# Gate stage of a graph network: one accumulator, eight places for gathered rows, loops of two turns, and an end without GpSimd

## The chip, the cores and the metric

One core of a Trainium2 chip runs the whole program. Its engines are TensorE (PE), VectorE (DVE), ScalarE (ACT), GpSimd (POOL) and SyncE (SP), each with its own stream of instructions; they meet at semaphores. The metric is the device time of one execution in microseconds; lower is better.

## The reference, cut to what matters

Four graph layers are applied one after the other to 6250 nodes of 128 features, with 100000 edges sorted by their target. The change touches the last one only, the gated layer:

```python
xr, xc = x[row], x[col]                       # source and target of each edge
x_src = xr @ W_src + b_src
x_dst = xc @ W_dst + b_dst
x_edge = concatenate([xr, xc]) @ W_edge + b_edge
gates = softmax(concatenate([x_src, x_dst, x_edge]) @ W_gate + b_gate)   # three gates of an edge
out = gates[:, 0:1] * x_src + gates[:, 1:2] * x_dst + gates[:, 2:3] * x_edge
result = x + segment_sum(out, col)            # summed by target node
```

## The kernel before

The stage before the loop computes, for each node, two vectors of 128 features and four logits (`p_gate`), and SyncE stores them as rows of 260 numbers in the table `tab_gate` in device memory. Then TensorE computes the products that belong to the target side (`p_gate_dst`, matmuls at line 1031, taken from PSUM by VectorE at line 1064), and the gate loop follows.

**The loop.** Edges are handled in steps of 128, four steps (`U`) are a part, four parts (`PARTS`) a turn. There are 52 turns, so 208 parts. `edge_loop` writes each engine's loop: a list of pairs (lag, step), run for each part, where a step with lag k handles the part that lies k parts back. The first turn is written out, 51 turns are a hardware loop (`Fori`), and the late parts are written out again. For each part:

- GpSimd (`gate_pool`, helper `gathers`, line 409) gathers the four steps' rows from `tab_gate` by source index, one indirect transfer for 128 rows, into `rows`. It has four places of a part, and the gathers of part n wait for `gate_msg` of part n - 4.
- SyncE loads the factors of the edges' places (`gate_sp`).
- TensorE (`gate_pe`) makes the one-hot matrices from them (`turn`, lines 1917 and 1919), multiplies the target logits by them (`logits`, line 1931, lag 1), and sums the messages into PSUM (`sums`, line 448, lag 3).
- ScalarE (`gate_act`) copies the one-hots out of PSUM (lines 1894 and 1897), takes exponentials (1888) and scales one half of the row (`scale`, 1902).
- VectorE (`gate_dve`) adds the gathered logits to the target ones (`logits`, line 1946, lag 2), forms the message of the part before (`message`, line 1969, lag 3), which posts `gate_msg`, divides the gates (`gates`, lag 2), and adds the four sums out of PSUM to the nodes' blocks (`step_add`, line 471, lag 4). It executes these in this order for each part.

**The two accumulators.** `Sums` adds even steps to `acc_flat` and odd steps to `h_flat`, the memory where the rows for the table stood. Two adds that follow each other could hit the same block, so an add waits for the completed ones before it; with two accumulators only every second add has such a wait:

```python
for u in range(U * at_once):
    if u % m == 0:
        dve.wait_ge(sem("win_added"), self.added0 + TURN + n + u)
```

where `m` is the number of accumulators. Both are cleared beforehand (line 2448, in the stage before, and line 1973).

**The end.** The nodes' blocks are handled in seven groups of seven blocks. VectorE adds the two accumulators (line 1982). ScalarE scales `t` by the second gate's sum (line 1851, 49 activations). GpSimd scales `w` by the third gate's sum and adds `x` (lines 2004 and 2008). VectorE adds the one term (1987) and the other (1990) and the group is stored.

The attention stage, two layers earlier, has a loop of the same kind. Its gathers (line 1350) go to eight places of a part (`KV_RING`), and wait for VectorE's line 1600.

Of the kernel before, what the change touches and what calls it, by code (L numbers as in the profile page):

```python
# [6 lines left out]
P = 128  # L7
# [10 lines left out]
U = 4  # L18
PARTS = 4
# [75 lines left out]
def edge_loop(engine, stages, turns=TURNS):  # L95


    for r in range(PARTS):
        for lag, step in stages:
            if r >= lag:  # L100
                step((r - lag) // PARTS, (r - lag) % PARTS)
    with engine.Fori(1, turns) as i:
        for r in range(PARTS):
            for lag, step in stages:
                back = (r - lag) // PARTS
                step(i + back if back else i, (r - lag) % PARTS)
    for late in range(max(lag for lag, _ in stages)):
        for lag, step in stages:
            if late < lag:
                step(turns + (late - lag) // PARTS, (late - lag) % PARTS)  # L110
# [35 lines left out]
def program(nc, a, out):  # L146
# [6 lines left out]
    with ExitStack() as ctx:  # L153
# [244 lines left out]
        GATHER_TURNS = (TURNS, TURNS)  # L398
        TURN0 = [sum(GATHER_TURNS[:k]) for k in range(len(GATHER_TURNS))]

        def gathers(pool, k, table, width, sources, free):

            for n in range(GATHER_TURNS[k] * PARTS):
                r = n % PARTS
                if n >= PARTS:
                    free(n - PARTS)
                for u in range(U):
                    at = n * U + u
                    pool.indirect_dma_start(rows[:, r * U + u, 0:width], None, table,  # L409
                                            bass.IndirectOffsetOnAxis(sources[:, at:at + 1], 0)).then_inc(rows_in[r], 16)  # L410

        class Sums:
# [24 lines left out]
            def step_pe(self, pe, message, arrived):  # L441
                def step(i, r):
# [9 lines left out]
            def step_add(self, dve, at_once=1):  # L452
# [5 lines left out]
                def step(i, r):  # L458
# [19 lines left out]
        ATT_PASS, GATE_PASS = 0, 1  # L478
        gate_sums = Sums(1, GATE_W, 4, 2, (acc_flat, h_flat))
# [449 lines left out]
        def group(v, g):  # L929
            return v[:, ds(g * GROUP, GROUP), :]  # L930
# [229 lines left out]
        ATT_TURN0 = TURN0[ATT_PASS]  # L1160
# [710 lines left out]

        def gate_pool(pool):
# [3 lines left out]
            gathers(pool, GATE_PASS, tab_gate, GATE_ROW, src_col, lambda n: pool.wait_ge(sem("gate_msg"), n + 1))  # L1876

        def gate_sp(sp):
            def load(i, r):
# [5 lines left out]
        def gate_act(act):  # L1885
            def exp(i, r):
# [3 lines left out]
            def copy(i, r):  # L1890
# [8 lines left out]
            def scale(i, r):  # L1899
                act.wait_ge(sem("gates_ready"), i * PARTS + r + 1)  # L1900
                for u in range(U):
                    last = nc.scalar.activation(scaled[:, u, :], rows[:, r * U + u, D:KV], ACT.Copy,  # L1902
# [9 lines left out]
        def gate_pe(pe):  # L1912
            def turn(i, r):
# [9 lines left out]
            def logits(i, r):  # L1923
# [16 lines left out]
        def gate_dve(dve, chain):  # L1940
            def logits(i, r):
# [3 lines left out]
                dve.wait_ge(rows_in[r], 16 * U * (GATE_TURN0 + i + 1))  # L1945
                nc.vector.tensor_tensor(z, banks(2 + r % RING2)[:, 0:4 * U].rearrange("p (u c) -> p u c", c=4),
                                        rows[:, r * U:(r + 1) * U, KV:GATE_ROW], ALU.add).then_inc(sem("gate_step"), 1)
# [6 lines left out]
            def gates(i, r):  # L1954
# [9 lines left out]
            def message(i, r):  # L1964
                n = i * PARTS + r
                dve.wait_ge(sem("gate_scaled"), n + 1)
                for u in range(U):
                    m = r * U + u
                    last = nc.vector.scalar_tensor_tensor(msg_gate[:, m, 0:D], rows[:, r * U + u, 0:D], msg_gate[:, m, D:D + 1],  # L1969
                                                          scaled[:, u, :], ALU.mult, ALU.add)  # L1970
                last.then_inc(sem("gate_msg"), 1)
            for flat in (acc_flat, h_flat):
                nc.vector.memset(flat[:, BLOCKS * D:BLOCKS * GATE_W], 0.0).then_inc(sem("gate_zeroed"), 1)
            dve.wait_ge(sem("gate_zeroed"), 2 * GROUPS + 2)
# [5 lines left out]
            sums, sums2 = by_block(acc_flat, BLOCKS, GATE_W), by_block(h_flat, BLOCKS, GATE_W)  # L1980
            with dve.Fori(0, GROUPS) as g:
                nc.vector.tensor_tensor(group(sums, g), group(sums, g), group(sums2, g), ALU.add).then_inc(sem("gates_summed"), 1)
# [520 lines left out]
```

## Time and profile before

| | |
|---|---|
| median of 3 runs | 6562.92 us (6562.47 to 6567.48) |
| profiled execution, its time | 6606.33 us |
| its span, first to last instruction | 6604.7 us |
| TensorE busy | 4142.5 us (63%) |
| VectorE busy | 2841.6 us (43%) |
| GpSimd busy | 2539.1 us (38%) |
| ScalarE busy | 1248.9 us (19%) |
| mean granted TensorE clock | 0.726 |

Times within the profile count from the first instruction's start. A row of a timeline gives start, duration, engine, line, operation, the tensors written and read, and in brackets the idle time before it with what ended it; "issue" is a wait for nothing that the profile shows, "remote" is a release by something it cannot name. The gate stage takes about the last 1470 us of the span.

### The profile page before, as it was taken

The page shows a single profiled execution, that of the slowest core. Times are in us where ns is not written, and L with a number is a line of the kernel's source. Part 1 is how long each engine was busy: PE and PEld are TensorE (multiplying, and loading weights), DVE is VectorE, ACT ScalarE, POOL GpSimd, SP SyncE. Part 2 cuts the span into 40 slices and gives each one's busy share as a digit, 9 for nine tenths or more (in the row PEclk, how much of TensorE's full clock was granted, in tenths as well). Part 3 has the DMA queues.
Part 4 walks back from the last instruction along what each step waited for, and adds up shares of the span by engine and source line. Part 5 has one row for each costly group of instructions (what it writes and reads, how often), then busy time and mean ns, then how long its engine had stood idle before and what let it go on. Part 6 is the DMA issues. An engine that isn't in the chain of part 4 may idle for free.

```text
span 6604.7 us, 89916 instructions
## 1 busy us (share of the span) xinstructions
PE 4142.5 (63%) x24308; PEld 3118.6 (47%) x24309; DVE 2841.6 (43%) x9274; ACT 1248.9 (19%) x3117; POOL 2539.1 (38%) x2543
## 2 busy tenths in 40 slices
PE   0000000059999965777777772999998777777765
PEld 0000000036656664666666652666666666666654
DVE  4343333451131144666666667313213444444446
ACT  0000000100010021222222223101001233333333
POOL 6677666300000035555556530000000455555555
PEclk6555555579999987888888875999999655555555
DMA  9811111035555445666666551455564232332222
GB/s 359 302 44 45 45 38 51 7 116 191 191 173 190 160 122 166 189 181 180 186 186 191 177 171 42 152 191 164 181 192 142 77 81 79 81 81 80 81 80 68
DMA packets 547602, 897.05 MB, mean 136 GB/s; under 512 B 99459, under 2 KB 401573, under 8 KB 541111
## 3 DMA queue, kind: packets, MB, share of 16 engines
q1 hardware_dynamic: 429558, 614.86, 29.2%
q0 software_dynamic: 106912, 224.30, 12.7%
q10 hardware_dynamic: 10912, 55.32, 2.3%
q8 instruction: 95, 1.56, 0.1%
q14 instruction: 125, 1.02, 0.1%
HBM read 734.69 MB, written 159.48 MB: 135 GB/s over the span
## 4 chain that ended last, share of the span: by engine, by line
PE 50%; issue 19%; DVE 14%; another core or an unknown queue 11%; ACT 3%; DVEq 2%; DMA 1%; SPq 1%; ACTq 0%; POOL 0%; POOLq 0%
PE ps L840 25%; DVE work L636 4%; PE ps L1931 4%; PE ps L1489 3%; PE ps L448 3%; PE ps L1502 3%; PE ps L1491 3%; PE ps L1031 2%; PE ps L1462 1%; DVE work L1969 1%; PE ps L847 1%; PE ps L1917 1%; PE ps L1468 1%; ACT work L1902 1%
## 5 line engine op out<-in xcount | busy, mean ns | idle before, releaser
L409 POOL DMA_INDIRECT work<-tab_gate,src_col x832 | 792.4, 952 | 1863.7 <-DMA tab_gate<-logits 1247.2
L1350 POOL DMA_INDIRECT work<-tab_kv,src_col x624 | 647.1, 1037 | 1656.1 <-PE ps L1031 1137.7
L515 POOL DMA_INDIRECT d_adj<-logits,address x782 | 779.3, 997 | 364.1 <-issue 239.9
L840 PE MATMUL ps<-hw 128*128 128x384 bf16 x5096 | 856.7, 328 | 41.6 <-DVE hw L819 34.1
L840 PE MATMUL ps<-hw,work 128*128 128x384 bf16 x5096 | 845.1, 326 | 0.0
L2226 PE MATMUL ps<-work 128*128 128x49 f32 x2 | 0.6, 418 | 1230.1 <-DVE work L2323 1230.1
L840 PEld LDWEIGHTS ps<-hw 128*128 128x128 bf16 x5096 | 500.7, 98 | 369.4 <-issue 33.7
L840 PEld LDWEIGHTS ps<-hw,work 128*128 128x128 bf16 x5096 | 498.8, 98 | 318.2
L885 DVE TENSOR_TENSOR work<-work,ps 128x128 f32 (+1 forms) x208 | 59.7, 287 | 1286.6 <-ACT work L872 1285.9
L2226 PEld LDWEIGHTS ps<-work 128*128 128x128 f32 x2 | 0.5, 313 | 1230.4 <-issue 1230.4
L448 PE MATMUL ps<-work 128*128 128x132 f32 x1664 | 436.5, 443 | 121.3 <-issue 75.1
L636 DVE SCALAR_TENSOR_TENSOR work<-hw,acc 128x256 bf16<-128x256 f32 x784 | 345.9, 484 | 310.9 <-issue 297.8
L448 PEld LDWEIGHTS ps<-work 128*128 128x128 f32 x1664 | 384.8, 334 | 124.7 <-issue 124.7
L1931 PEld LDWEIGHTS ps<-logits,work 128*128 128x128 f32 x1664 | 370.2, 327 | 42.3 <-issue 42.3
L1931 PE MATMUL ps<-logits,work 128*128 x1664 | 388.0, 356 | 0.2
L872 ACT ACTIVATE work<-ps 128x128 f32 x208 | 57.6, 277 | 1683.4 <-PE ps L840 1683.4
L1564 DVE TENSOR_TENSOR acc<-acc,ps 128x136 f32 x832 | 240.0, 288 | 231.9 <-remote 142.8
L1902 ACT ACTIVATE work<-work 128x128 f32<-128x128 f32 x832 | 265.7, 390 | 272.9 <-DVE work L1961 185.4
L1489 PE MATMUL ps<-weights,work 128*128 128x128 f32 x1664 | 304.6, 339 | 12.9 <-issue 11.5
L1489 PEld LDWEIGHTS ps<-weights,work 128*128 128x128 f32 x1664 | 259.6, 238 | 78.0 <-issue 78.0
L1917 PE MATMUL ps<-step_rows,node_factors 6*128 6x512 bf16 x208 | 124.8, 600 | 269.6 <-ACT work L1897 246.4
L1491 PE MATMUL ps<-t,work 128*128 x1664 | 279.1, 321 | 17.8 <-issue 17.8
(435 smaller groups left out, 6221.2 us busy)
## 6 DMA issues: line engine op xcount, KB each, us to landing
hw<-d_adj SPq DMA_DIRECT2D x104, 800.0 KB, 4.3
work<-d_adj SPq DMA_DIRECT2D x104, 800.0 KB, 4.4
d_adj<-acc SPq DMA_DIRECT2D x52, 1568.0 KB
hw<-d_adj SPq DMA_DIRECT2D x104, 768.0 KB, 4.2
work<-d_adj SPq DMA_DIRECT2D x104, 768.0 KB, 4.3
work<-attr_dram SPq DMA_DIRECT2D x832, 64.0 KB
hw<-d_keys ACTq DMA_DIRECT2D x49, 1024.0 KB
hw<-d_value SPq DMA_DIRECT2D x192, 256.0 KB
```

The source lines that it names most:

```text
L409: pool.indirect_dma_start(rows[:, r * U + u, 0:width], None, table, bass.IndirectOffsetOnAxis(sources[:, at:at + 1], 0)).then_inc(rows_in[ ...
L448: nc.tensor.matmul(self.place(r, u), hot[:, r * U + u, :], message(r, u), start=True, stop=True).then_inc(sem("win_done"), 1)
L515: pool.indirect_dma_start(d_adj, bass.IndirectOffsetOnAxis(address[:, tile:tile + 1], 0), counts[:, tile:tile + 1], None).then_inc(adj_out ...
L636: ins = nc.vector.scalar_tensor_tensor(same[:, k, :], key_rows[:, half, k // 2, :], key_col[:, at], weigh[:, k % 2, :], ALU.is_equal, ALU. ...
L840: last = nc.tensor.matmul(at, adj_half[2 * s + hf][:, k, :], xs[:, b, :], start=b == 0, stop=b == BLOCKS - 1)
L1350: pool.indirect_dma_start(kv_rows[r][:, at % U, :], None, tab_kv, bass.IndirectOffsetOnAxis(src_col[:, at:at + 1], 0)).then_inc(rows_in[r] ...
L1489: nc.tensor.matmul(e[:, u * D:(u + 1) * D], attr_t[:, r % RING2, u * D:(u + 1) * D], weight("L1_We"), start=True, stop=True)
L1491: last = nc.tensor.matmul(q[:, u * D:(u + 1) * D], hot_t[:, r % RING2, u * P:(u + 1) * P], t[:, ds(blocks[u], 1), :].rearrange("p b f -> p ...
L1502: nc.tensor.matmul(sum_place(6, u), hot_sum[:, r * U + u, :], msg_att[:, r * U + u, :], start=True, stop=True).then_inc(sem("win_done"), 1)
L1564: nc.vector.tensor_tensor(nodes, nodes, place, ALU.add).then_inc(sem("win_added"), 1)
L1902: last = nc.scalar.activation(scaled[:, u, :], rows[:, r * U + u, D:KV], ACT.Copy, scale=msg_gate[:, r * U + u, GATE2:GATE2 + 1])
L1931: last = nc.tensor.matmul(banks(2 + r % RING2)[:, u * 4:u * 4 + 4], hot_t[:, r % RING2, u * P:(u + 1) * P], logits_dst[:, ds(blocks[u], 1) ...
```

## The change

- `Sums` gets one accumulator, `acc_flat`, so every add waits for the one before. `h_flat` is not cleared any more.
- The gathers get eight places: parts of even turns go to `rows`, those of odd turns to the memory of `h_flat` (`gate_rows`). The gathers of part n wait for the message of part n - 8, and there are eight semaphores for arrivals.
- `edge_loop` writes two turns into the hardware loop's body, since the place now depends on the turn's parity (`half`). Two turns are written out before it, and the loop runs 25 times.
- At the end, ScalarE scales both `t` and `w` (98 activations), VectorE adds the two terms and `x` (three adds a group), and GpSimd does nothing.

```diff
 def edge_loop(engine, stages, turns=TURNS):
-    for r in range(PARTS):
+    def steps(p, turn, pair, begin):
         for lag, step in stages:
-            if r >= lag:
-                step((r - lag) // PARTS, (r - lag) % PARTS)
-    with engine.Fori(1, turns) as i:
-        for r in range(PARTS):
-            for lag, step in stages:
-                back = (r - lag) // PARTS
-                step(i + back if back else i, (r - lag) % PARTS)
+            q = p - lag
+            if q >= begin:
+                step(turn + q // PARTS, q % PARTS, pair + q // (2 * PARTS), q // PARTS % 2)
+    for p in range(2 * PARTS):
+        steps(p, 0, 0, 0)
+    with engine.Fori(1, turns // 2) as pair:
+        for p in range(2 * PARTS):
+            steps(p, pair * 2, pair, -2 * PARTS)
...
-        gate_sums = Sums(1, GATE_W, 4, 2, (acc_flat, h_flat))
+        gate_sums = Sums(1, GATE_W, 4, 2)
...
+        gate_rows = [rows, part(h_flat, 0, (TURN, GATE_ROW))]
...
-            gathers(pool, GATE_PASS, tab_gate, GATE_ROW, src_col, lambda n: pool.wait_ge(sem("gate_msg"), n + 1))
+            for n in range(ALL_PARTS):
+                if n >= KV_RING:
+                    pool.wait_ge(sem("gate_msg"), n - KV_RING + 1)
+                for at in range(n * U, (n + 1) * U):
+                    pool.indirect_dma_start(gate_rows[n // PARTS % 2][:, n % PARTS * U + at % U, :], None, tab_gate,
+                                            bass.IndirectOffsetOnAxis(src_col[:, at:at + 1], 0)).then_inc(rows_in[n % KV_RING], 16)
...
-                dve.wait_ge(rows_in[r], 16 * U * (GATE_TURN0 + i + 1))
+                dve.wait_ge(rows_in[half * PARTS + r], 16 * U * (GATE_TURN0 + pair + 1))
...
-            with dve.Fori(0, GROUPS) as g:
-                nc.vector.tensor_tensor(group(sums, g), group(sums, g), group(sums2, g), ALU.add).then_inc(sem("gates_summed"), 1)
-            with chain.loop(GROUPS, 1) as g:
+            with chain.loop(GROUPS, 2) as g:
                 dve.wait_ge(sem("gate1_part"), g + 1)
                 at = group(sums, g)[:, :, 0:D]
                 chain.after(nc.vector.tensor_tensor(at, at, group(t, g), ALU.add))
                 dve.wait_ge(sem("gate2_part"), g + 1)
-                nc.vector.tensor_tensor(group(x, g), at, group(w, g), ALU.add).then_inc(sem("out_ready"), 1)
+                chain.after(nc.vector.tensor_tensor(at, at, group(w, g), ALU.add))
+                nc.vector.tensor_tensor(group(x, g), at, group(x, g), ALU.add).then_inc(sem("out_ready"), 1)
...
+            act.wait_ge(sem("win_added"), gate_sums.added0 + TURN + STEPS)
             with act.Fori(0, GROUPS) as g:
                 scale_nodes(act, g, t, ..., "gate1_part")
+                scale_nodes(act, g, w, ..., "gate2_part")
-        def gate_end_pool(pool):
...
-                for flat in (acc_flat, h_flat):
-                    nc.vector.tensor_copy(flat[:, ds(g * GROUP * D, GROUP * D)], ...)
+                nc.vector.tensor_copy(acc_flat[:, ds(g * GROUP * D, GROUP * D)], ...)
```

## Rows read from the trace of the kernel before

**Rows 1.** Windows: the loop's steady part and the end after it.

```profile
core 0: us, PE busy (x) PEld busy (x) DVE busy (x) ACT busy (x) POOL busy (x), PEclk, DMA share, GB/s
5176.20:6541.50 1365.30, 979.84 (x4293) 823.52 (x4292) 602.12 (x2855) 504.68 (x1431) 776.80 (x816) 0.50 0.30 80
6553.80:6604.70 50.90, 0.00 (x0) 0.00 (x0) 44.07 (x21) 14.86 (x49) 35.69 (x14) 0.50 0.22 63
```

**Rows 2.** Timeline of TensorE, one turn in the middle of the loop.

```profile
5861.04 0.60 PE L1917 MATMUL ps<-step_rows,node_factors 6*128 6x512 bf16 x1 [0.62 <-ACT work L1897]
...
5863.73 2.11 PE L448 MATMUL ps<-work 128*128 128x132 f32 x8
5865.77 0.60 PE L1917 MATMUL ps<-step_rows,node_factors 6*128 6x512 bf16 x1
...
5876.86 0.60 PE L1917 MATMUL ps<-step_rows,node_factors 6*128 6x512 bf16 x1 [6.30 <-ACT work L1897]
```

**Rows 3.** Timeline of VectorE, the same stretch.

```profile
5863.09 0.29 DVE L471 TENSOR_TENSOR acc<-acc,ps 128x132 f32 x1 [0.60 <-issue]
5863.30 0.28 DVE L471 TENSOR_TENSOR hw<-hw,ps 128x132 f32 x1
5863.72 0.29 DVE L471 TENSOR_TENSOR acc<-acc,ps 128x132 f32 x1
...
5875.06 0.29 DVE L471 TENSOR_TENSOR acc<-acc,ps 128x132 f32 x1 [8.81 <-remote]
...
5876.43 0.17 DVE L1946 TENSOR_TENSOR small<-ps,work 128x16 f32<-128x16 f32 x1 [0.24 <-issue]
...
5880.20 0.17 DVE L1946 TENSOR_TENSOR small<-ps,work 128x16 f32<-128x16 f32 x1
```

**Rows 4.** Timeline of GpSimd, the same stretch: first and last of twelve gathers, and the next.

```profile
5858.49 0.94 POOL L409 DMA_INDIRECT work<-tab_gate,src_col  x1 [3.63 <-DVE work L1969]
...
5872.60 0.94 POOL L409 DMA_INDIRECT work<-tab_gate,src_col  x1 [0.30 <-issue]
5878.34 0.94 POOL L409 DMA_INDIRECT work<-tab_gate,src_col  x1 [4.80 <-DVE work L1969]
```

**Rows 5.** Waits of GpSimd and VectorE, 5176 to 6553 us: total, times, longest.

```profile
POOL work L409 <- DVE work L1969: 386.7, 89, 23.4
...
DVE acc L471 <- remote: 228.6, 34, 8.8
```

**Rows 6.** Attention stage, eight places: waits of GpSimd; VectorE's timeline after a burst.

```profile
POOL work L1350 <- DVE hw L1600: 344.9, 82, 21.2
...
2424.96 1.09 DVE L1080 SCALAR_TENSOR_TENSOR t<-ps,biases 128x896 f32<-128x896 f32 x1 [11.01 <-remote]
```

**Rows 7.** First burst of the gate stage: timelines; windows of TensorE in and after it.

```profile
5151.90 0.95 POOL L409 DMA_INDIRECT work<-tab_gate,src_col  x1 [0.30 <-issue]
...
5154.95 1.09 DVE L1064 TENSOR_TENSOR hw<-ps,biases 128x896 f32<-128x896 f32 x1 [9.49 <-remote]
...
5145.45:5152.50 7.05, 3.47 (x14) 0.80 0.39 103
5156.10:5166.05 9.95, 9.84 (x70) 0.81 0.01 2
```

**Rows 8.** Timelines of ScalarE and VectorE in the end.

```profile
6555.27 6.25 ACT L1851 ACTIVATE t<-t,acc  x21 [5.75 <-DVE acc L1982]
6561.73 2.16 ACT L1851 ACTIVATE t<-t,acc  x7 [0.22 <-issue]
...
6590.83 2.95 DVE L1987 TENSOR_TENSOR acc<-acc,t  x1
...
6595.07 1.08 DVE L1987 TENSOR_TENSOR acc<-acc,t  x1
6596.43 1.09 DVE L1990 TENSOR_TENSOR x<-acc,hw  x1 [0.28 <-DVE acc L1987]
...
6598.81 1.09 DVE L1990 TENSOR_TENSOR x<-acc,hw  x1 [0.28 <-DVE acc L1987]
```

**Rows 9.** Transfers by issue: size, and median us from issue to landing.

```profile
hw<-d_adj SPq DMA_DIRECT2D x104, 768.0 KB, 4.2
```

More of the change, by code:

```diff
@@ L109, in edge_loop @@
             if late < lag:
-                step(turns + (late - lag) // PARTS, (late - lag) % PARTS)
+                n = turns * PARTS + late - lag
+                step(n // PARTS, n % PARTS, n // (2 * PARTS), n // PARTS % 2)
 def pair_loop(engine, count, step):
@@ L393, in registers @@
             return values
[L398 to L410, printed above, removed]
         class Sums:
@@ L441, in step_pe, with step @@
             def step_pe(self, pe, message, arrived):
-                def step(i, r):
+                def step(i, r, pair, half):
                     self.hot_made(pe, i, r)
@@ L456, in step_add, with step @@
                 blocks = []
-                def step(i, r):
+                def step(i, r, pair, half):
                     n = U * (i * PARTS + r)
@@ L1885, in gate_act, with exp, copy @@
         def gate_act(act):
-            def exp(i, r):
+            def exp(i, r, pair, half):
                 act.wait_ge(sem("gate_in"), i * PARTS + r + 1)
                 nc.scalar.activation(gate_exp[r % RING2], gate_z[r % RING2], ACT.Exp).then_inc(sem("gate_exp"), 1)
-            def copy(i, r):
+            def copy(i, r, pair, half):
                 n = i * PARTS + r
@@ L1897, in copy, with scale @@
                 nc.scalar.activation(hot[:, r * U:(r + 1) * U, :], banks(1), ACT.Relu, bias=1.0, scale=-1.0).then_inc(sem("gate_copied"), 1)
-            def scale(i, r):
+            def scale(i, r, pair, half):
                 act.wait_ge(sem("gates_ready"), i * PARTS + r + 1)
                 for u in range(U):
-                    last = nc.scalar.activation(scaled[:, u, :], rows[:, r * U + u, D:KV], ACT.Copy,
+                    last = nc.scalar.activation(scaled[:, u, :], gate_rows[half][:, r * U + u, D:KV], ACT.Copy,
                                                 scale=msg_gate[:, r * U + u, GATE2:GATE2 + 1])
@@ L1912, in gate_pe, with turn @@
         def gate_pe(pe):
-            def turn(i, r):
+            def turn(i, r, pair, half):
                 n = i * PARTS + r
@@ L1921, in turn, with logits @@
                 last.then_inc(sem("gate_turned"), 1)
-            def logits(i, r):
+            def logits(i, r, pair, half):
                 n = i * PARTS + r
@@ L1940, in gate_dve, with logits @@
         def gate_dve(dve, chain):
-            def logits(i, r):
+            def logits(i, r, pair, half):
                 n, z = i * PARTS + r, gate_z[r % RING2]
                 dve.wait_ge(sem("gate_logits"), n + 1)
-                dve.wait_ge(rows_in[r], 16 * U * (GATE_TURN0 + i + 1))
+                dve.wait_ge(rows_in[half * PARTS + r], 16 * U * (GATE_TURN0 + pair + 1))
                 nc.vector.tensor_tensor(z, banks(2 + r % RING2)[:, 0:4 * U].rearrange("p (u c) -> p u c", c=4),
-                                        rows[:, r * U:(r + 1) * U, KV:GATE_ROW], ALU.add).then_inc(sem("gate_step"), 1)
+                                        gate_rows[half][:, r * U:(r + 1) * U, KV:GATE_ROW], ALU.add).then_inc(sem("gate_step"), 1)
                 dve.wait_ge(sem("gate_step"), 4 * n + 1)
@@ L1952, in logits, with gates @@
                                         ALU.subtract).then_inc(sem("gate_in"), 1)
[L1954 removed]
+            def gates(i, r, pair, half):
                 n, e = i * PARTS + r, gate_exp[r % RING2]
@@ L1962, in gates, with message @@
                                         gate_max[r % RING2].unsqueeze(2).broadcast_to((P, U, 3)), ALU.mult).then_inc(sem("gates_ready"), 1)
-            def message(i, r):
+            def message(i, r, pair, half):
                 n = i * PARTS + r
```

28 lines of the change are left out of this document (7 added, 21 removed).

## The prediction

> **What bounds the kernel now.** I read the stage windows first. The gate loop's steady part, from 5176.2 to 6541.5 us, takes 1365.3 us for 204 parts (816 gathers by 4), 6.69 us a part, and no engine fills it: TensorE is busy 72%, GpSimd 57%, VectorE 44% [rows 1]. TensorE runs at a granted clock of 0.50, the 1.2 GHz level, throughout. Then the end after the loop: 50.9 us in which TensorE does nothing.
>
> Then I laid three timelines of one stretch side by side. TensorE goes through a part in 4.73 us when nothing stops it (L1917 at 5861.04 and 5865.77) [rows 2]. VectorE needs about 3.8 us a part: its logits at 5876.43 come again at 5880.20 [rows 3]. GpSimd needs four gathers, 4 x (0.95 + 0.30) = 5.0 us. Each would allow 5.0 us a part or less, yet the part takes 6.69. The difference is a wait in common. TensorE's sums L448 were recorded at 5863.73 to 5865.84, but VectorE, which adds them, starts only at 5875.06, after 8.81 us idle that the profile puts to "remote", to nobody it knows [rows 2, 3]. TensorE itself waits on until 5876.86, for a copy by ScalarE that was late in the same way. GpSimd's timeline shows what ends at that moment: twelve gathers without a break from 5858.49, the last issued at 5872.60 and over at 5873.54. Its next begins at 5878.34, after VectorE's message [rows 4]. So I read: some 5 us into a burst of gathers, what TensorE has finished reaches the others late, and it gets through about 2 us after the burst's last gather. Then VectorE makes a message, which frees a place, and the next burst starts. This repeats: GpSimd waits for VectorE 89 times, 386.7 us in all, and VectorE's adds wait 34 times for "remote", 228.6 us [rows 5]. The cycle is then 1.25 us a gather plus about 4.8 us of idle: twelve gathers in 19.85 us, 6.6 us a part.
>
> What sets the time of a part is therefore how many messages fall into one burst, and the gap between bursts. It is not whether a gathered row is there in time.
>
> **The change, part by part.**
>
> *Eight places instead of four.* A gather still waits for a message, only for one that is four parts older. In the steady loop GpSimd has filled the ring and stands waiting, with four places as with eight: each message releases four gathers. I cost it there at nothing. The cover for that is in the attention stage, which already has eight places. There GpSimd waits for VectorE 82 times in one of its two groups, 344.9 us, so extra places did not remove the stop [rows 6]. The ring acts at the two ends of the stage.
>
> Start: the first burst grows from 16 gathers (until 5151.90 + 0.95) to 32, 16 x 1.25 = 20.0 us longer. In the old burst VectorE stood idle 9.49 us for TensorE's product and went on at 5154.95, 2.1 us after the burst [rows 7]; the attention stage shows the same with 11.01 us idle [rows 6]. The products of the destination logits come before the loop, and GpSimd's longest wait for a message, 23.4 us [rows 5], lies between this burst and the loop's first message, so this is on the path. The hold is not complete: 14 matmuls in 7.05 us got through in it, against 70 in 9.95 us after it [rows 7]. Over 20 us about 40 get through, worth 40 x 0.142 = 5.7 us. Cost +14.3 us. Bounds: 0 (if a longer burst holds nothing more) and +20.0.
>
> Tail: the last gather is issued four parts earlier, so four parts run at TensorE's 4.73 instead of 6.69: 4 x 1.96 = -7.8. The last four parts run at VectorE's pace with its slower adds, 4 x 0.42 = +1.7. Together -6.1. Bounds -8 and 0.
>
> *One accumulator.* Each add now waits for the add before it, where only every second did. The row shows both: from the first add to the second 0.21 us (independent), from the second to the third 0.42 us (5863.09, .30, .72) [rows 3]. Two of four steps go from 0.21 to 0.42, and so does the step from the fourth of one part to the next part's first, where other work lies between anyway: 0.42 us a part at most. In the middle of a burst this is hidden under GpSimd, since a message each 3.8 + 0.4 = 4.2 us still comes before the four gathers of 5.0 us are issued. It is on the path where the adds are the first thing after a burst: 34 times "remote" [rows 5], 34 x 0.42 = +14.3. Bounds: 0, and every burst, 89 x 0.42 = +37. I take the 34, since the row counts the case.
>
> *Loops of two turns.* 25 of 50 back-edges go. VectorE shows 0.24 us idle at one (5876.43) and none at the same step elsewhere (5880.20) [rows 3], with loop registers about 0.3. It is on the path only where a burst's end meets the loop's end, 34 / 4 = 8.5 times, half of them removed: -1.3. Bounds -7.5 (25 x 0.3) and 0.
>
> *Clearing.* The second accumulator's copy (0.54 us to the next start) and memset (0.2) before the products and the loop: -0.8; the other six lie under waits for transfers.
>
> *The end.* Before, from 6553.8: VectorE adds the two sums, ScalarE scales one term, GpSimd scales and adds x, and VectorE's adds take 2.95 us while GpSimd runs (6590.83) and 1.08 when it is still (6595.07); the last ends at 6599.90 [rows 8]: 46.1 us. After: ScalarE makes 98 activations. The row of 21 takes 6.25 us, of which the last is 0.39 long: 5.86 / 20 = 0.293 each, and 0.22 between groups [rows 8]. 98 x 0.293 + 7 x 0.22 = 30.3. VectorE makes three adds a group: 1.36 + 1.36 + 1.01 = 3.7 us from 6595.07, 6596.43 and so on, less than ScalarE's 4.3, so ScalarE sets the pace, and two adds follow the last scaling: 1.36 + 1.09 = 2.5. With 0.3 to start, 33.1 us; -13.0. Bounds: -16 (if the activations go at 0.26) and +10 if VectorE's adds stay at 2.95 with ScalarE beside them (7 x 8 us).
>
> On that last bound the Trainium skill has a rule ("SBUF — State Buffer", SBUF: two separate sides): only VectorE and GpSimd share ports, and ScalarE has its own. By that rule VectorE's adds take 1.08 us and the end saves 13.0; without it the bound of +10 would stay open. The fall from 2.95 to 1.08 us when GpSimd stops agrees.
>
> Sum: 14.3 - 6.1 + 14.3 - 1.3 - 0.8 - 13.0 = +7.4 us. The profiled execution took 6606.3 us (span 6604.7 and 1.6 around it), so it becomes 6613.7. The median of the runs is 6562.9, 43 us less; I carry the difference over unchanged: 6570.3, say 6570 us. A measurement can tell 0.2%, 13 us, so this is no change.
>
> **Rivals.**
>
> A. *The places do lengthen the bursts* (faster). If GpSimd falls behind in the ring and catches up, a burst could hold four messages: 16 gathers, 20.0 + 4.8 = 24.8 us for four parts, 6.2 a part instead of 6.69: 200 x 0.49 = -98 us, 6472. At the limit GpSimd never stops, 5.0 a part: -338, 6232. For it: GpSimd is the slowest engine of a part, and a deeper ring is what lets it run on. Against it: the attention stage has the places and stops as often [rows 6]. It decides from the point where a third message in a burst of eight would no longer be held. Chance 0.12.
>
> B. *The start and the adds cost nothing* (slightly faster): the longer first burst does not delay the products, and the adds hide. 7.4 - 28.6 = -21, 6542. For it: TensorE still gets on in a burst. Chance 0.16.
>
> C. *The adds come onto every cycle* (slower): after each burst VectorE has adds before its message. +37 instead of +14.3: 6593. For it: a slower VectorE drifts behind TensorE, so more adds are left over. Chance 0.14.
>
> D. *Code* (slower): the doubled body leaves an engine's instruction store, and each of 25 back-edges waits for a transfer. No back-edge here shows such a wait on VectorE. The nearest row is a transfer's time to landing, 4.2 us [rows 9]; 25 x 4.2 = 105, half of it hidden in the holds: +52, 6622. It decides when the body of VectorE, which I count at about 120 instructions of engine and sequencer a turn and so about 250 for two, is too long. Chance 0.10.
> The Trainium skill ("Advanced Engine Details and Errata", ISA Cache) gives two lines of 256 instructions to an engine other than TensorE. By that 250 just fit and the cost is 0; if a line is dropped at the crossing it is D. No row here tells.
>
> **How the numbers follow.** My forecast, all terms as summed, has 0.48: 6570, between 6555 and 6585. A 0.12, B 0.16, C 0.14, D 0.10. Faster by over 0.2% (below 6550): A, B and a little of the forecast's spread, 0.30. Within 0.2%: 0.40, nearly all the forecast's. Slower (above 6576): C, D and the forecast's upper edge, 0.30. The range takes in B, C and D and leaves A out: 6535 to 6620.
>
> **What would show it.** First burst of 32 gathers, with VectorE idle more than 20 us in it before the destination products go on, and the loop starting near 5182 rather than 5167. Gathers still in groups of 8 and 12 with 3.5 to 5 us between, at about 6.75 us a part. Adds 0.42 us apart. The end 33 us plus the store. No wait at VectorE's back-edge. The prediction is wrong if the groups of gathers grow to 16 or more, if the first burst leaves the products alone, or if VectorE's adds in the end are not near 1.1 us.

## The result, and the profile after

The changed kernel takes 6587.09 us in the median of 20 runs (6569.66 to 6604.17); the kernel before, run beside it, takes 6569.4 us (6562.4 to 6586.77). The ratio is 1.0023 [1.0016, 1.0030]: some 15 us more (10 to 20). I had forecast 6570 us, 7.4 us more, as the likeliest, and 6535 to 6620 as the range. So the time lies in the range, but above the 6555 to 6585 that I had given to my own sum. The change is slower, and its interval lies on both sides of the 0.2% that I had called the limit; "no change" had been the likelier outcome by its chance.

The two profiled executions seem to say the opposite: the span of after is 6588.9 us, that of before 6604.7. The stages ahead of the gate stage, which the change leaves alone, were 26 us shorter in this execution: VectorE's first destination product is at 5106.93 us, and at 5133.19 us in before. So I compare the gate stage alone, from that product to the end of the span. It takes 1482.0 us after and 1471.5 us before, 10.5 us more, which is at the lower end of what the ratio allows. Its parts, each read from the first and last rows of the timelines:

| us | before | after | difference | predicted |
|---|---|---|---|---|
| destination products, to the small memset | 34.6 | 56.5 | +21.9 | +13.5 (start, clearing) |
| from there to the first gather that a message releases | 8.5 | 9.1 | +0.6 | 0 |
| 200 parts of the loop (6.693 and 6.708 each) | 1338.5 | 1341.6 | +3.1 | +13.0 (adds, loops) |
| the rest to the last add (four more parts before) | 38.8 | 38.5 | -0.3 | -6.1 (tail) |
| the end | 51.2 | 36.3 | -14.9 | -13.0 |
| all | 1471.5 | 1482.0 | +10.5 | +7.4 |

Here is the start, first in VectorE's timeline of the kernel after, then in GpSimd's.

```profile
5106.93 1.08 DVE L1046 TENSOR_TENSOR hw<-ps,biases 128x896 f32<-128x896 f32 x1
...
5121.19 1.09 DVE L1046 TENSOR_TENSOR t<-ps,biases 128x896 f32<-128x896 f32 x1 [5.97 <-remote]
5136.65 1.09 DVE L1046 TENSOR_TENSOR hw<-ps,biases 128x896 f32<-128x896 f32 x1 [14.37 <-remote]
5152.10 1.09 DVE L1046 TENSOR_TENSOR t<-ps,biases 128x896 f32<-128x896 f32 x1 [14.36 <-remote]
...
5163.41 0.07 DVE L1962 MEMSET work<- 128x16 f32 x1
```

```profile
5107.00 0.95 POOL L1863 DMA_INDIRECT work<-tab_gate,src_col  x1 [1241.51 <-DMA tab_gate<-logits]
...
5145.75 0.95 POOL L1863 DMA_INDIRECT hw<-tab_gate,src_col  x1 [0.30 <-issue]
5172.56 0.94 POOL L1863 DMA_INDIRECT work<-tab_gate,src_col  x1 [25.87 <-DVE work L1957]
```

The first burst holds 32 gathers without a break, from 5107.00 to 5146.70, where [rows 7] had 16. From 8.2 us into it (5115.22) VectorE waits for TensorE's products: 5.97, 14.37 and 14.36 us, one product in between each. In before it had one wait of this kind, 9.49 us. The last of these waits ends 5.4 us after the burst; the loop's first message ends GpSimd's 25.87 us of idle time. TensorE's timeline shows that these products had been ready, as far as its own rows go:

```profile
5108.16 10.40 PE L1013 MATMUL ps<-weights,t 128*128 128x128 f32 x69 [4.02 <-DVE hw L1046]
5118.94 0.27 PE L1013 MATMUL ps<-weights,t 128*128 128x128 f32 x1 [0.38 <-issue]
```

The stage has 196 matmuls for 14 products, 14 each. Three products were made before these rows, so their 70 matmuls are the fourth to the eighth product, over at 5119.21. VectorE takes the sixth at 5121.19, the seventh at 5136.65 and the eighth at 5152.10, 32.9 us after its last matmul.

The loop's steady part and the end, as windows (the columns are those of [rows 1]); below them waits in the loop: total, times, longest.

```profile
5172.50:6514.20 1341.70, 962.09 (x4198) 806.65 (x4196) 619.75 (x2784) 494.41 (x1397) 762.80 (x800) 0.50 0.30 80
6552.70:6588.90 36.20, 0.00 (x0) 0.00 (x0) 22.39 (x21) 28.73 (x98) 0.00 (x0) 0.50 0.31 88
```

```profile
POOL work L1863 <- DVE work L1957: 225.3, 49, 25.9
POOL hw L1863 <- DVE work L1957: 157.0, 39, 6.4
```

Eight places or four, GpSimd stops for VectorE's messages just as often: 49 + 39 = 88 times, 382 us, against 89 times and 386.7 us in [rows 5]. The clock is at the 1.2 GHz level (0.50) here too. A stretch of the loop in VectorE's timeline, and in GpSimd's:

```profile
5870.07 1.60 DVE L454 TENSOR_TENSOR acc<-acc,ps 128x132 f32 x4 [0.59 <-issue]
5874.13 0.17 DVE L1934 TENSOR_TENSOR small<-ps,work 128x16 f32<-128x16 f32 x1 [2.46 <-remote]
...
5882.22 1.60 DVE L454 TENSOR_TENSOR acc<-acc,ps 128x132 f32 x4 [5.97 <-remote]
...
5901.67 0.17 DVE L1934 TENSOR_TENSOR small<-ps,hw 128x16 f32<-128x16 f32 x1 [0.33 <-issue]
```

```profile
5864.91 0.94 POOL L1863 DMA_INDIRECT hw<-tab_gate,src_col  x1 [3.61 <-DVE work L1957]
...
5873.66 0.95 POOL L1863 DMA_INDIRECT work<-tab_gate,src_col  x1 [0.30 <-issue]
5876.03 0.94 POOL L1863 DMA_INDIRECT work<-tab_gate,src_col  x1 [1.43 <-DVE work L1957]
...
5885.64 0.95 POOL L1863 DMA_INDIRECT work<-tab_gate,src_col  x1 [4.92 <-DVE work L1957]
```

Four adds take 1.60 us, so they start 0.44 apart ((1.60 - 0.29) / 3); the first three of before start 0.21 and 0.42 apart [rows 3]. The bursts still hold eight gathers (5864.91 to 5874.61), four (from 5876.03) or twelve. The row at 5901.67 is the back-edge of VectorE's loop, 0.33 us; the next one is eight parts later, at 5956.36. All 24 of them in the trace have a gap of at most 0.64 us from the branch to the next instruction, 0.29 in the median.

The end, in the timeline of both engines, from the last add of the loop:

```profile
6551.94 0.72 DVE L454 TENSOR_TENSOR acc<-acc,ps 128x132 f32 x2
6552.97 2.15 ACT L1832 ACTIVATE t<-t,acc  x7 [6.15 <-DVE acc L454]
6555.03 2.14 ACT L1832 ACTIVATE hw<-hw,acc  x7
6555.50 1.09 DVE L1972 TENSOR_TENSOR acc<-acc,t  x1 [2.84 <-ACT t L1832]
...
6557.40 1.09 DVE L1975 TENSOR_TENSOR acc<-acc,hw  x1 [0.81 <-ACT hw L1832]
...
6583.14 1.09 DVE L1976 TENSOR_TENSOR x<-acc,x  x1
```

ScalarE goes on without a gap, 4.09 us a group; VectorE waits for it and ends at 6584.2, 31.6 us after the last add.

### The profile page after: what moved, and what is told of

Its sections match the earlier page's. It is cut to its first block, busy times and chain, and to the rows that moved or that the text cites. A ratio compares the mean times of both kernels' runs of the same rounds, so it can differ in the third digit from the quotient of the medians.

```text
span 6588.9 us, 89987 instructions
## 1 busy us (share of the span) xinstructions
PE 4148.8 (63%) x24308; PEld 3118.9 (47%) x24309; DVE 2850.7 (43%) x9266; ACT 1264.4 (19%) x3166; POOL 2504.9 (38%) x2529
## 4 chain that ended last, share of the span: by engine, by line
PE 49%; issue 19%; DVE 15%; another core or an unknown queue 11%; ACT 3%; DVEq 2%; DMA 1%; ACTq 0%; SPq 0%; POOL 0%; POOLq 0%
PE ps L822 25%; DVE work L618 4%; PE ps L1470 3%; PE ps L1483 3%; PE ps L1919 3%; PE ps L1472 3%; PE ps L1013 2%; PE ps L431 2%; DVE work L1957 2%; PE ps L1443 2%; PE ps L829 1%; DVE acc L454 1%; PE ps L1449 1%; PE ps L1905 1%
## 5 line engine op out<-in xcount | busy, mean ns | idle before, releaser
L1863 POOL DMA_INDIRECT work<-tab_gate,src_col x416 | 397.1, 955 | 1579.8 <-DMA tab_gate<-logits 1241.5
L822 PE MATMUL ps<-hw 128*128 128x384 bf16 x5096 | 857.1, 329 | 38.8 <-DVE hw L801 30.8
L822 PEld LDWEIGHTS ps<-hw 128*128 128x128 bf16 x5096 | 500.4, 98 | 367.3 <-issue 33.1
L1863 POOL DMA_INDIRECT hw<-tab_gate,src_col x416 | 395.9, 952 | 275.8 <-DVE work L1957 157.0
L454 DVE TENSOR_TENSOR acc<-acc,ps 128x132 f32 x832 | 242.8, 292 | 459.9 <-remote 269.3
```

Of the source, the lines that this page charges most:

```text
L454: nc.vector.tensor_tensor(nodes, nodes, self.place(r + u // U, u % U), ALU.add).then_inc(sem("win_added"), 1)
L822: last = nc.tensor.matmul(at, adj_half[2 * s + hf][:, k, :], xs[:, b, :], start=b == 0, stop=b == BLOCKS - 1)
L1863: pool.indirect_dma_start(gate_rows[n // PARTS % 2][:, n % PARTS * U + at % U, :], None, tab_gate, bass.IndirectOffsetOnAxis(src_col[:, at ...
```

## The experiments

The result leaves two theories of what the eight places do. In the first, mine, TensorE's completions come late while gathers by index run, so that a long first burst costs and a deeper ring gives nothing. In the other it is the traffic, or the order of the work, that holds TensorE up, and the places matter elsewhere. The single edits were tried beside them, each on its own, since +10.5 us is made of terms that cancel. All ratios are against the kernel before on the same chip: 20 runs of after, 11 or 12 of each of the others.

| kernel | ratio to before | products | us a part | tail, from the last gather | end | stage |
|---|---|---|---|---|---|---|
| before | 1 | 34.6 | 6.693 | 12.0 | 51.2 | 1471.5 |
| after | 1.0023 [1.0016, 1.0030] | 56.5 | 6.708 | 38.5 | 36.3 | 1482.0 |
| after, ring of four | 0.9992 [0.9980, 1.0004] | 34.9 | 6.712 | 16.8 | 36.3 | 1466.3 |
| after, first burst of 16 | 1.0003 [0.9989, 1.0016] | 35.3 | 6.730 | 33.0 | 36.3 | 1478.1 |
| before, new end | 0.9976 [0.9963, 0.9988] | 36.2 | 6.681 | 15.0 | 37.9 | 1460.1 |
| before, one accumulator | 1.0042 [1.0028, 1.0057] | 36.3 | 6.834 | 21.7 | 45.6 | 1505.7 |
| before, loops of two turns | 0.9999 [0.9987, 1.0011] | 36.5 | 6.682 | 12.9 | 51.0 | 1472.4 |
| before, accumulator and loops | 1.0021 [1.0006, 1.0035] | 34.1 | 6.728 | 18.5 | 45.6 | 1478.9 |
| before, new end, loops | 0.9971 [0.9956, 0.9986] | 34.7 | 6.659 | 12.1 | 37.7 | 1451.3 |
| before, new end, three places | 0.9984 [0.9971, 0.9996] | 30.1 | 6.698 | 10.9 | 37.8 | 1460.0 |
| before, new end, loops, three places | 0.9982 [0.9972, 0.9992] | 30.1 | 6.688 | 11.0 | 37.6 | 1457.9 |

All but the ratios is in us. The stage is that of one profiled execution each, yet its difference to before agrees with the ratio within 7 us everywhere.

**The ring's depth.** After, with the wait of the ring of four:

```diff
-                if n >= KV_RING:
-                    pool.wait_ge(sem("gate_msg"), n - KV_RING + 1)
+                if n >= PARTS:
+                    pool.wait_ge(sem("gate_msg"), n - PARTS + 1)
```

> The changed kernel, but the gathers of part n wait for the message of part n - 4 instead of n - 8, so only four places are ever filled ahead; the first burst is 16 gathers again. My theory (places do nothing in the loop, the long first burst delays the destination products): the products take 34 us again instead of 56.2, the loop stays at 6.71 us a part within 0.03, and the whole is 20 us (17 to 24) below the changed kernel, so 5 to 10 below the kernel before. Rival (the places help in the loop, and the loss is elsewhere): the loop gets slower than 6.75 us a part and the gain is below 10 us.

The ratio falls from 1.0023 to 0.9992, 20 us by the ratios and 15.7 in the stage. Windows of the steady part and the end:

```profile
5146.20:6515.52 1369.32, 982.76 (x4294) 824.68 (x4292) 635.27 (x2854) 506.60 (x1430) 779.73 (x816) 0.50 0.30 80
6532.36:6568.63 36.27, 0.00 (x0) 0.00 (x0) 22.40 (x21) 28.73 (x98) 0.00 (x0) 0.50 0.31 88
```

816 gathers are 204 parts, 6.712 us each, as with eight places. The products take 34.9 us instead of 56.5. So the ring's depth does nothing in the loop and costs 22 us at the start. It gives 5 us back at the end: eight places have four parts less in the loop (26.8 us) and a tail of 38.5 instead of 16.8.

**The first burst alone.** The eight places stay, and the fifth part's gathers wait until TensorE has come to its first part of the loop:

```diff
             for n in range(ALL_PARTS):
+                if n == 4:
+                    pool.wait_ge(sem("gate_turned"), 1)
```

> The changed kernel, but the gathers of parts 4 to 7 wait until TensorE has made the loop's first turn, so the first burst is 16 gathers and 16 more follow at the loop's start. My theory: the products take 34 us, 22 less; the 16 gathers, 20 us long, now hold TensorE at the loop's start, so most of it comes back there: 0 to 10 us below the changed kernel. Rival (only the overlap with the products hurts, and a burst at the loop's start is hidden since places are full): the whole 22 us stay, 18 to 24 below the changed kernel.

```profile
5122.76 1.09 DVE L1046 TENSOR_TENSOR hw<-ps,biases 128x896 f32<-128x896 f32 x1 [8.12 <-remote]
```

VectorE's timeline shows one wait for "remote" in the products, of 8.12 us, and they take 35.3 us. But the sixteen gathers that were put off now hold up the loop's first messages in a burst of 20 there, where VectorE waits up to 18.3 us. Of the 21 us gained at the products 3.9 are left in the stage (the ratios have 13, with intervals that allow 4). So the same burst costs time at the loop's start too.

**The new end.** In before, GpSimd's part goes, ScalarE scales both terms, and VectorE makes three adds a group; the sum of the two accumulators stays.

```diff
-            with chain.loop(GROUPS, 1) as g:
+            with chain.loop(GROUPS, 2) as g:
...
-                nc.vector.tensor_tensor(group(x, g), at, group(w, g), ALU.add).then_inc(sem("out_ready"), 1)
+                chain.after(nc.vector.tensor_tensor(at, at, group(w, g), ALU.add))
+                nc.vector.tensor_tensor(group(x, g), at, group(x, g), ALU.add).then_inc(sem("out_ready"), 1)
...
+                scale_nodes(act, g, w, lambda b: sums[:, ds(b, 1), GATE2:GATE2 + 1].rearrange("p b f -> p (b f)"), "gate2_part")
```

> The kernel before with the new end alone: VectorE still adds the two accumulators first, then ScalarE scales both terms and VectorE makes three adds a group; GpSimd does nothing. The end took 51.1 us before and 36.2 in the changed kernel. My theory (ScalarE sets its pace at 4.3 us a group): 38 us, 11 to 15 below the kernel before. Rival (the gain of the end came from the missing sum of accumulators, not from GpSimd's absence): 44 us or more, under 7 below.

The ratio is 0.9976 [0.9963, 0.9988], the end 37.9 us instead of 51.2. The timeline of its beginning:

```profile
6535.97 7.31 DVE L1982 TENSOR_TENSOR acc<-acc,hw  x7 [0.27 <-DVE hw L471]
6537.40 2.16 ACT L1851 ACTIVATE t<-t,acc  x7 [6.62 <-DVE acc L1982]
```

VectorE sums all seven groups first (7.31 us), and ScalarE starts 1.4 us into that: the end is ScalarE's 98 activations again. One accumulator saves only another 1.6 us here (36.3).

**One accumulator and the loops.** In before:

```diff
-        gate_sums = Sums(1, GATE_W, 4, 2, (acc_flat, h_flat))
+        gate_sums = Sums(1, GATE_W, 4, 2)
...
-            with dve.Fori(0, GROUPS) as g:
-                nc.vector.tensor_tensor(group(sums, g), group(sums, g), group(sums2, g), ALU.add).then_inc(sem("gates_summed"), 1)
+            dve.sem_inc(sem("gates_summed"), GROUPS)
```

> The kernel before with one accumulator alone; the second is still cleared but not used, and the end has no sum of the two (GpSimd and ScalarE start at once). By my prediction's term the loop costs 14.3 us more (0.42 us at 34 bursts); by the changed kernel's trace, which has 6.71 us a part against 6.69, about 4 more. The end, without the first sums, 5 to 10 us less. So +5 by the prediction's term, -3 by the trace, against the kernel before. Rival (every cycle pays): +25 or more.

```profile
5135.33:6529.52 1394.19, 978.98 (x4284) 821.09 (x4282) 633.27 (x2840) 505.19 (x1425) 778.69 (x816) 0.50 0.29 78
6551.18:6596.74 45.56, 0.00 (x0) 0.00 (x0) 34.17 (x14) 14.42 (x49) 34.51 (x14) 0.50 0.24 70
```

The window of the loop is 28.9 us longer than that of before, 6.834 us a part, and the tail another 9.7; the end gives 5.6 back. The whole kernel is 28 us slower (18 to 37). This is near rival C's price, not my +14.3. The waits of its loop say where it sits:

```profile
POOL work L409 <- DVE work L1969: 413.0, 85, 24.6
DVE acc L471 <- remote: 347.7, 52, 8.6
```

The adds wait for "remote" 52 times, against 34 before.

The loops alone, before with the new `edge_loop`, and both together. (The steps take `pair` and `half` and don't use them.)

```diff
...
+    for p in range(2 * PARTS):
+        steps(p, 0, 0, 0)
+    with engine.Fori(1, turns // 2) as pair:
+        for p in range(2 * PARTS):
+            steps(p, pair * 2, pair, -2 * PARTS)
...
```

> The kernel before with loops of two turns alone. By my prediction's term 1.3 us less (VectorE's back-edge shows only where a burst ends on it), the loop at 6.69 us a part. Rival: loops of two turns are what gave back the adds' cost in the changed kernel (6.71 us a part there, against 6.83 with one accumulator alone), so they are worth 0.1 us a part: 6.59, 20 us or more below the kernel before.

> The kernel before with one accumulator and loops of two turns, four places in one memory. One accumulator alone took 6.83 us a part. If the loops of two turns gave the adds' cost back, this shows 6.71, as the changed kernel does, and 10 us or less over the kernel before. If they do not, it stays at 6.80 to 6.86, 20 to 35 us over, and what gave it back is the second memory, or the order of bursts has a spread of its own.

The loops alone: 0.9999 [0.9987, 1.0011], 6.682 us a part; nothing to measure, as -1.3 us can't be. Both together: 1.0021 [1.0006, 1.0035], 6.728 us a part, which is 14 us over the kernel before, between the two outcomes that I had set. So the accumulator costs 14 us on two-turn loops and 28 on one-turn ones by the ratios, and the intervals overlap. This kernel has four places in one memory, and its part is within 0.02 us of that of after (6.708), of the ring of four (6.712) and of the first burst of 16 (6.730). So neither the number of places nor the second memory keeps the adds' cost down in after. The bursts between 5200 and 6480 us show what the time is made of. A burst ends where GpSimd is idle for over 0.6 us; each cell is the number of bursts and the mean from one's start to the next one's:

| gathers in the burst | 4 | 8 | 12 |
|---|---|---|---|
| before | 7, 9.65 us | 60, 13.00 us | 21, 20.33 us |
| before, loops | 9, 9.44 | 55, 12.83 | 24, 20.28 |
| before, one accumulator | 13, 10.04 | 43, 12.57 | 28, 20.93 |
| before, accumulator and loops | 20, 10.11 | 55, 12.09 | 19, 20.77 |
| after | 17, 9.94 | 59, 12.31 | 18, 20.75 |

A burst of twelve is 0.42 to 0.6 us longer with one accumulator: there the adds are first after it, and the chained add shows at the price that I took from [rows 3]. But the bursts of eight become 0.4 to 0.9 us shorter, and there are more bursts of four, which cost 10 us for one part. How much is left depends on the mix, and the mix seems to differ between the two forms of the loop (28 twelves against 19). That difference leans on the border: with 1.0 us of idle time in place of 0.6 the twelves are 27, 32, 37, 33 and 29 down the table, while the longer twelves, the shorter eights and the additional fours stay. Whether and why the loop's form shifts the mix, these runs don't settle; a drift between engines of a few tenths of a microsecond a turn could do it, and so could chance in one execution each.

**Fewer places.** If the depth of the ring does nothing, three places should do. Three places make the first burst 12 gathers. Before with the new end, with the wait three parts back:

```diff
-                if n >= PARTS:
-                    free(n - PARTS)
+                if n >= places:
+                    free(n - places)
```

> The kernel before with the new end, and the gathers of part n wait for the message of part n - 3, so three places are filled ahead. My theory (places do nothing in the loop, each part in the first burst delays the products): the loop stays at 6.68 us a part within 0.05, the first burst is 12 gathers and the products take 3 to 5 us less than 36: 3 to 5 below the new end alone. Rival (places matter once they are few): rows come late for VectorE's logits and the loop is slower by 0.2 us a part or more, 40 us.

VectorE's timeline at the start, and waits of the stage:

```profile
5097.73 1.09 DVE L1064 TENSOR_TENSOR hw<-ps,biases 128x896 f32<-128x896 f32 x1 [4.61 <-remote]
```

```profile
POOL work L409 <- DVE work L1969: 379.4, 102, 3.8
DVE small L1946 <- remote: 260.8, 102, 3.8
```

The wait in the products falls to 4.61 us and the products to 30.1. In the loop the bursts are all of eight gathers (102 waits, none over 3.8 us), and each takes 13.4 us: 6.698 us a part. With four places and the same edits beside it (new end alone) the part took 6.681 us in mixed bursts, so neither the fourth place nor the mix matters much. The 3 to 5 us that I expected to gain didn't come: the stages are equal (1460.0 and 1460.1 us). The products gain 6.1, and the slower part (3.5) and the last gathers, which are issued a part later (2.6), take them back; the ratio, 0.9984 against 0.9976, shows no gain either.

**Gathers by index, or bytes?** After, with each gather bringing 64 of the row's 260 numbers:

```diff
-                    pool.indirect_dma_start(gate_rows[n // PARTS % 2][:, n % PARTS * U + at % U, :], None, tab_gate,
+                    pool.indirect_dma_start(gate_rows[n // PARTS % 2][:, n % PARTS * U + at % U, 0:64], None, tab_gate,
```

> The changed kernel, but each gather brings 64 of the 260 numbers of a row (the rest of a place keeps what was there, so the gates and messages are of other data). As many gathers, a quarter of the bytes. If the hold on TensorE belongs to GpSimd's stream of gathers and not to the bytes: about 6.7 us a part, the products 56 us. If it belongs to the bytes: the part falls to GpSimd's 5.0 us, the products to 25 us, and the whole by 340 us or more.

And after with a plain load of as many bytes from the same queue in the place of each gather; it brings other rows than the edges ask for:

```diff
-                for at in range(n * U, (n + 1) * U):
-                    pool.indirect_dma_start(gate_rows[n // PARTS % 2][:, n % PARTS * U + at % U, :], None, tab_gate,
-                                            bass.IndirectOffsetOnAxis(src_col[:, at:at + 1], 0)).then_inc(rows_in[n % KV_RING], 16)
+                b = n % (BLOCKS - U)
+                for u in range(U):
+                    pool.dma_start(gate_rows[n // PARTS % 2][:, n % PARTS * U + u, :],
+                                   node_rows(tab_gate)[:, b + u, :]).then_inc(rows_in[n % KV_RING], 16)
```

> The changed kernel, but in place of a gather by index GpSimd issues a plain load of 128 consecutive rows of the table (other rows than the edges ask for, so another result). As many transfers from the same queue, the same bytes, no index. If the hold belongs to every transfer from GpSimd: VectorE's waits for remote stay and the part takes over 6 us. If it belongs to gathers by index: no such waits, TensorE's 4.73 us a part, the loop 400 us shorter.

Of the narrow gathers, the window of 1300 us in the loop and the start in VectorE's timeline; then waits in that window:

```profile
5200.00:6500.00 1300.00, 919.39 (x4045) 773.05 (x4045) 603.34 (x2705) 475.62 (x1352) 734.67 (x771) 0.50 0.13 20
```

```profile
5121.37 1.09 DVE L1046 TENSOR_TENSOR t<-ps,biases 128x896 f32<-128x896 f32 x1 [6.01 <-remote]
5141.04 1.09 DVE L1046 TENSOR_TENSOR hw<-ps,biases 128x896 f32<-128x896 f32 x1 [18.58 <-remote]
5152.30 1.09 DVE L1046 TENSOR_TENSOR t<-ps,biases 128x896 f32<-128x896 f32 x1 [10.17 <-remote]
```

```profile
DVE small L1934 <- remote: 306.0, 86, 5.0
```

20 GB/s instead of 80, and the times stay: 6.720 us a part, 56.2 us for the products, 6588.71 us in all. Only the mix is another, nearly all bursts of eight, which once more leaves the part as long as it was.

Of the plain loads, a window of 700 us, and a row of each engine's timeline in it:

```profile
5300.00:6000.00 700.00, 700.00 (x3112) 594.20 (x3110) 467.56 (x2075) 363.31 (x1036) 314.64 (x592) 0.50 0.40 114
```

```profile
5603.21 2.12 POOL L1864 DMA_DIRECT2D hw<-tab_gate  x4 [2.61 <-DVE work L1958]
```

```profile
5604.01 1.59 DVE L454 TENSOR_TENSOR acc<-acc,ps 128x132 f32 x4 [0.60 <-issue]
```

More bytes than ever, 114 GB/s, and TensorE is busy for all of the 700 us: 4.713 us a part. No wait in that stretch is put to "remote". The products take 21.6 us and the kernel 6148.95 us, 440 less than the narrow gathers in one run each. In the loop the four loads take GpSimd only 2.1 us a part in place of 5.0, so nearly all its bursts there are shorter than the 4.3 us after which, at the earliest, a burst of gathers in before holds anything up. The first burst is the fair comparison: 32 loads in 17.1 us without a break, beside the same products. GpSimd's, VectorE's and TensorE's rows of it, and its window:

```profile
5100.85 8.61 POOL L1864 DMA_DIRECT2D work<-tab_gate  x16 [1243.21 <-DMA tab_gate<-logits]
5109.38 8.59 POOL L1864 DMA_DIRECT2D hw<-tab_gate  x16
5114.95 1.09 DVE L1046 TENSOR_TENSOR t<-ps,biases 128x896 f32<-128x896 f32 x1 [0.47 <-PE ps L1013]
5102.19 18.87 PE L1013 MATMUL ps<-weights,t 128*128 128x128 f32 x154 [3.84 <-DVE hw L1046]
5100.85:5117.97 17.12, 15.78 (x128) 15.81 (x129) 11.92 (x12) 0.00 (x0) 17.12 (x32) 0.90 0.79 225
```

From the fourth on the products come 1.56 us apart, TensorE's 154 matmuls have no gap, and the rate is 225 GB/s, where the first burst of after has 104. A load and a gather of whole rows have 48 packets each. So the hold belongs to the gathers by index, and bytes, packets or a busy queue of GpSimd don't make it. What in such a gather does, its reading of the index or the work on GpSimd behind it, no run here tells.

**The best of both.** Before with the new end and the new loops, and the same with three places:

> The kernel before with the new end and loops of two turns, two accumulators, four places. The new end alone was 0.24% below the kernel before, with the end at 37.9 us. My term for the loops gives 1 us more: 0.25% below. If the loops are worth 0.1 us a part, 0.5 to 0.6% below, and this is the best version.

> The kernel before with the new end, loops of two turns, two accumulators, and three places of rows filled ahead. From the stage times of the parts measured so far: products 30 us (three places), loop 6.68 us a part, end 37.7: 0.25 to 0.4% below the kernel before. A rival is that three places cost what the products gain, as the whole time with three places alone suggests: then 0.2% or less.

The first has 0.9971 [0.9956, 0.9986], 6560.91 us, the lowest of all; before with the new end alone is within its interval. Three places save 4.6 us at the start, and their loop is 29 thousandths of a microsecond a part longer (6.688 against 6.659): 0.9982 [0.9972, 0.9992], no better. The gain at the start did not add up to a faster kernel; by the ratio itself the rival came, 0.2% or less below before.

## Why the prediction was right in the sum, and where it was not

**The cause of the bound: right.** I read a hold of TensorE's completions by a burst of gathers out of three timelines. The narrow gathers keep it. The plain loads end it, in a burst of 32 too, and the part falls to TensorE's 4.7 us [rows 2].

**Places cost nothing in the loop, rival A falls.** Parts of 6.708 and 6.712 us with eight and four places show it, and 6.681 and 6.698 with four and three before the accumulator's change. A's bursts of 16 never came.

**The start: the term was mis-sized.** I priced it at +14.3 us, with a bound of +20.0, and it was +22.1 (21.9, and 0.2 for the memset that went). The step that failed is "over 20 us about 40 get through, worth 5.7 us". In the last 20 us of the burst, 5126.70 to 5146.70, TensorE's timeline has 11 matmuls, less than one product. My rate came from TensorE's 14 matmuls in 7.05 us [rows 7], which it made while it still had a place in PSUM to write to. In the longer burst it runs out of them: finished products reach VectorE one in 15 us, and its next matmuls come only after VectorE has taken one (5137.89 after 5136.65). The last result came at 5152.10, 5.4 us after the burst rather than 2.1, which takes it over my bound. With 11 matmuls and this delay in my own sum it is 20.0 - 11 x 0.142 + 3.3 = +21.7.

**The tail: the term was mis-sized.** -6.1 us predicted, -0.3 measured. The experiments part it in two, one profiled execution each. The places alone (ring of four against after) give -5.1, where I had -7.8. The adds alone cost +4.8 (12.0 in before, 16.8 with the ring of four), where I had +1.7. The last gather of after, in GpSimd's timeline, and what VectorE has left to do then:

```profile
6513.18 0.94 POOL L1863 DMA_INDIRECT hw<-tab_gate,src_col  x1 [0.30 <-issue]
```

```profile
6516.21 1.60 DVE L454 TENSOR_TENSOR acc<-acc,ps 128x132 f32 x4 [6.55 <-remote]
6517.83 0.17 DVE L1934 TENSOR_TENSOR small<-ps,work 128x16 f32<-128x16 f32 x1
...
6543.38 0.17 DVE L1934 TENSOR_TENSOR small<-ps,hw 128x16 f32<-128x16 f32 x1
```

The hold of the last burst goes on for 2.1 us after it, and seven of VectorE's logits rows (L1934) are left, 4.26 us apart; in the ring of four two are left. So five parts are added where I counted four: 5 x 4.26 = 21.3 us for the 26.8 that four parts take in the loop. The adds' part is the late first message after that hold (3.5 us behind the last gather in the ring of four, 1.0 in before, which had no hold there) and 0.45 and 1.8 us in the steps behind it. One step of my working failed in each: the parts in flight at the last gather, and a hold at the end of the last burst, which I had left out.

**The adds: right in place, wrong in effect.** I took 34 x 0.42 = +14.3. Alone they cost 28.9 us in the loop, near rival C's 37. In after they and the loops cost 3.1. What I had right is the price of a twelve, +0.42 to +0.6; what I had not is that the bursts of eight shorten and the mix moves. So the step that failed is "34 x 0.42": the count of the waits doesn't stay as it is when the adds get longer. All four kernels with these adds on two-turn loops take 6.708 to 6.730 us a part, and only the one with one-turn loops takes 6.834. Whether the loop's form does that or chance does stays open.

**Loops and code: right.** -1.3 us predicted, 0.9999 [0.9987, 1.0011] alone. Rival D falls: VectorE's body of two turns has 250 instructions by the trace, and its back-edge is the 0.33 us of the row at 5901.67, where a turn of 118 had 0.24 [rows 3]; no wait of a transfer's length is there. The Trainium skill's two lines of 256 instructions ("Advanced Engine Details and Errata", ISA Cache) agree with that; no run here has a body that doesn't fit.

**The end: right.** -13.0 predicted, -14.9 in after and -13.3 alone. 33.1 us were predicted for the part up to VectorE's last add, and 31.6 were measured: ScalarE has no gap between its groups. VectorE's adds take 1.08 to 1.09 us with ScalarE busy beside them, where GpSimd beside them made it 2.95 [rows 8]. The Trainium skill ("SBUF — State Buffer", SBUF: two separate sides) has the rule that VectorE shares ports with GpSimd and not with ScalarE. The trace agrees, with 1.08 us against 2.95.

In all, +21.9 + 0.6 + 3.1 - 0.3 - 14.9 = +10.4; the ratio says 15 (10 to 20), twice my +7.4. That the sum came out this near was luck, because my errors cancelled: I had 8 us too little for the start and 6 us too much gain in the tail, but 10 us too much for adds and loops and 2 us too little gain at the end.

## What to carry to other kernels

A deeper prefetch ring did nothing in a loop whose data wasn't late. Where the queue is stopped by the consumer's turn, look at both ends of the loop: there the ring's depth is the length of a burst that other work has to stand through.

When two engines wait together and the profile names nobody, lay the timelines side by side and look for what a third engine does at that moment. Then price an edit by which instruction is first after the stall. Test the terms one by one: here a gain of 13 us at the end was hidden by a loss of 22 at the start in the same change, and undoing the one kept the other.

## What was not expected of the hardware

While GpSimd issues gathers by index back to back, results of TensorE reach VectorE and ScalarE late. In the loop of before the earliest such wait begins 4.3 us into a burst, and most end 1.5 to 2.6 us after its last gather; after the burst of 32 it was 5.4 us. It doesn't depend on the bytes (6.708 us a part at 80 GB/s, 6.720 at 20), and it isn't there with plain loads from the same queue (4.713 us a part at 114 GB/s, and no wait for "remote" beside a burst of 32 loads at 225 GB/s). In a burst of 32 gathers one product came through in 15 us. The loop's part takes 6.7 us where GpSimd's four gathers need 5.0, so I estimate the hold at 1.7 us a part, 340 us in the loop, and 35 us in the products. The rest of the 440 us that the plain loads save is mostly the step from GpSimd's 5.0 us a part to TensorE's 4.7.

One gather of 128 rows takes GpSimd 0.95 us and 0.30 us to the next, for rows of 260 numbers and of 64 alike; a plain load takes it 0.54 us.
